# One-core transformer layer: attention weighs two key blocks side by side, takes its denominators from GpSimd sums and gives its score banks out in rotation

## What is computed

```python
kqv = x @ Wqkv + bqkv
kqv = kqv.reshape(b, s, 3, NUM_HEADS, HEAD_SIZE)      # 16 heads of 32
...
scores = jnp.einsum('bsnh,btnh->bnst', k, q) / math.sqrt(HEAD_SIZE)
ones = jnp.ones_like(scores)
scores = jnp.triu(scores) + -10000.0 * jnp.tril(ones, k=-1)
attn = jax.nn.softmax(scores, axis=2)
out = jnp.einsum('bnkq,bknh->bqnh', attn, v)
out = out.reshape(b, s, NUM_HEADS * HEAD_SIZE)
return out @ Wo + bo
```

## Time and profile before

| what | value |
|---|---|
| times of three runs | 3363.21, 3372.99 and 3378.21 us |
| median | 3372.99 us |
| the profiled execution: its own time | 3368.79 us |
| the profiled execution: its span | 3367.1 us |
| mean granted clock of TensorE, as a share of full speed | 0.936 |
| busy shares: PE, DVE, ACT, POOL | 91%, 66%, 33%, 22% |
| attention of the first batch | from about 168 us to 427 us of the span |

### The profile page before, as it was taken

One profiled execution on the slowest core, in us unless ns is written; L12 is line 12 of the kernel. 1 busy time (PEld: TensorE's weight loads), 2 busy tenths in 40 slices (PEclk: granted clock), 3 DMA queues, 4 the chain that ended last, 5 costly groups with the idle time before them and its releaser, 6 DMA issues.

```text
span 3367.1 us, 59590 instructions
## 1 busy us (share of the span) xinstructions
PE 3061.7 (91%) x20772; PEld 2095.2 (62%) x20772; DVE 2211.2 (66%) x2961; ACT 1102.6 (33%) x1728; POOL 752.8 (22%) x1065
## 2 busy tenths in 40 slices
PE   3599999999879998999978999999997999999998
PEld 3445457777555446777755544777774454577775
DVE  1356667777646667777764675777764566677776
ACT  1123314444113333344311332344421233143441
POOL 3301102333031111233311110133322011013330
PEclk6779999999879999999987999999998799999999
DMA  7422202111131211111121220111112222021111
GB/s 229 144 47 69 51 1 64 44 48 56 48 82 44 63 32 34 43 49 51 41 83 44 63 63 14 54 41 48 45 48 77 51 69 51 1 64 43 48 57 48
DMA packets 160038, 189.48 MB, mean 56 GB/s; under 512 B 43834, under 2 KB 103866, under 8 KB 158074
## 3 DMA queue, kind: packets, MB, share of 16 engines
q1 hardware_dynamic: 155998, 173.74, 18.6%
q0 software_dynamic: 2720, 10.49, 0.8%
q10 hardware_dynamic: 1152, 3.15, 0.4%
HBM read 104.90 MB, written 23.36 MB: 38 GB/s over the span
## 4 chain that ended last, share of the span: by engine, by line
PE 76%; DVE 9%; issue 4%; DMA 4%; SPq 3%; ACT 2%; POOL 1%; DVEq 0%; ACTq 0%; POOLq 0%
PE ps L700 13%; PE ps L702 12%; PE ps L701 12%; PE ps L844 7%; PE ps L809 6%; PE ps L827 5%; PE ps L1000 4%; PE ps L886 3%; PE ps L986 2%; PE ps L745 2%; PE ps L1046 2%; DVE LM L1558 2%; PE ps L710 1%; DVE mneg L1466 1%; PE ps L1009 1%
## 5 line engine op out<-in xcount | busy, mean ns | idle before, releaser
L700 PE MATMUL ps<-uh,win 128*128 128x512 f32 x1536 | 629.8, 410 | 4.1 <-POOL win L1719 3.4
L702 PE MATMUL ps<-uh,win 128*128 128x512 f32 x1536 | 605.3, 394 | 0.0
L701 PE MATMUL ps<-ul,win 128*128 128x512 f32 x1536 | 602.4, 392 | 0.0
L1466 DVE TENSOR_REDUCE mneg<-ps 128x1 f32<-128x128 f32 (+7 forms) x512 | 363.5, 752 | 179.1 <-PE ps L812 173.6
L1175 ACT ACTIVATE PR<-ps 128x1024 f32<-128x1024 f32 (+3 forms) x384 | 310.2, 809 | 412.4 <-PE ps L830 275.0
L700 PEld LDWEIGHTS ps<-uh,win 128*128 128x128 f32 x1536 | 290.9, 189 | 95.8 <-issue 29.6
L844 PE MATMUL ps<-PR,VG 128*32 128x512 f32 (+3 forms) x1536 | 339.6, 519 | 10.8 <-DVE OS L1472 8.3
L846 PE MATMUL ps<-PR,ones 128*32 128x512 f32 (+3 forms) x1536 | 339.6, 519 | 0.0
L702 PEld LDWEIGHTS ps<-uh,win 128*128 128x128 f32 x1536 | 290.0, 189 | 65.3
L1582 DVE TENSOR_TENSOR LM<-ps,LM 128x512 f32<-128x512 f32 x256 | 170.2, 686 | 243.1 <-PE ps L1000 197.3
L701 PEld LDWEIGHTS ps<-ul,win 128*128 128x128 f32 x1536 | 291.4, 190 | 54.9
(11 more groups left out here) (216 smaller groups left out, 5162.1 us busy)
## 6 DMA issues: line engine op xcount, KB each, us to landing
...
QS<-EV SPq DMA_DIRECT2D x192, 128.0 KB, 2.4
KS<-EV SPq DMA_DIRECT2D x168, 128.0 KB, 2.4
...
edec<-ed_t SPq DMA_DIRECT2D x512, 16.0 KB, 1.6
```

The lines of the kernel that those rows point to most:

```text
L700: pe.matmul(dst, hi_l, hi_r, start=first, stop=False)
L701: pe.matmul(dst, hi_l, lo_r, start=False, stop=False)
L702: return pe.matmul(dst, lo_l, hi_r, start=False, stop=last)
L1466: dve.tensor_reduce(mneg[:, hh, t:t + 1], wide(b0)[:, 0:(t + 1) * P], AX.X, ALU.max, negate=True).then_inc(a_max.sem, 1)
```

## The change

- `scores_b` now goes through the units in plain order. `weigh` takes two units (a pair, k = 0 to 5) at a time: unit 2k in the column groups 0 and 1, unit 2k+1 in 2 and 3. The products with ones are gone from it. DVE's `take` adds the two parts: one or two copies from PSUM and an addition, for each of the two column halves c.
- POOL adds up the probabilities of a half into `acc` (`sums`, ten steps, each after the unit's exponential), and PE makes the denominators of both column halves from it with four matmuls side by side (`denominators`), once in a half, after pair 0 of the next half; for p7 within `row_product`, after its first row block. ACT copies them to `rec`, DVE inverts them in two steps of 128 x 256 and multiplies (`scale`), which POOL did before. The low part of the weights (`group_lo`) also moves from POOL to DVE.
- PR has four tiles. The exponential of unit u waits for POOL's sum and PE's weighing of unit u-4.
- The banks 0 to 5 are three slots of two banks, given out in rotation to all score jobs: units ("b"), row blocks of `scores_a` ("a", 16 blocks packed into ten jobs by `TILES`) and transposes of maxima ("t"). A job waits for the reader of the job three places ahead of it (`slot_free`).
- The maxima are turned in two steps of 8 rows (t0 and t1); their DMAs, two each, are issued by ACT. The first two units of the next half stand in `TAIL`. SP stacks queries and keys of the next group in two portions.
- The first group and the last stand outside of the loop, which the program before did for the last alone. Semaphores of loads and stores are merged (`s_tile`).

```diff
-ORDER = [(0, 0), (0, 3), (0, 2), (0, 1), (1, 0), (1, 7), (1, 6), (1, 5), (1, 4), (1, 1), (1, 2), (1, 3)]
+ORDER = [(c, s) for c in range(2) for s in range(4 * c + 4)]
 UNITS = len(ORDER)
-
-SCORE_BANK = [2, 4, 2] + [4] * 7 + [2, 4]
-
-BANK_FREE = [-1, 0, 1, 2, 4, 5, 6, 7, 8, 9, 3, 10]
-
-
-AHEAD = {2: (0, 1, 2, 3), 3: (4, 5), 4: (6, 7), 5: (8, 9, 10, 11), 6: (12, 13), 7: (14, 15)}
-TURN_AT = 9
-PROJECT_AT = (4, 6, 8, 10)
-
-MAX_BANK = [0, 1, 2, 3, 0, 2, 0, 2]
-MAX_FREE = [-1, -1, 0, 0, 2, 4, 5, 6]
+PAIRED = UNITS // 2
...
+TILES = [[(0, 3, 0), (0, 2, 512), (0, 0, 896)], [(1, 3, 0), (1, 2, 512), (1, 0, 896)],
+         [(0, 4, 0), (0, 1, 640)], [(1, 4, 0), (1, 1, 640)],
+         [(0, 5, 0)], [(1, 5, 0)], [(0, 6, 0)], [(1, 6, 0)], [(0, 7, 0)], [(1, 7, 0)]]
+
+AT = [[], [("a", 0), ("a", 1)], [("a", 2), ("a", 3), ("a", 4)], [("t", 0), ("a", 5), ("a", 6), ("a", 7)], [("a", 8), ("a", 9)], []]
+TAIL = [("b", 12), ("b", 13), ("t", 1)]
+SUMMED = [1, 1, 2, 3, 4, 4, 5, 6, 7, 8, 9, 10]
...
+BODY = [j for k in range(PAIRED) for j in units_of(k) + AT[k]] + TAIL
+CLOSE = [j for k in range(PAIRED) for j in units_of(k)]
+OPEN = [("a", i) for i in range(5)] + [("t", 0)] + [("a", i) for i in range(5, 10)] + TAIL
...
+            if i >= 3:
+                self.before[j] = (jobs[i - 3], 0)
+            elif earlier:
+                self.before[j] = (earlier[i - 3], 1)
...
-            PR = sb("PR", [P, 2, 2, HB], at=c)
-            mneg = sb("mneg", [P, 2, TT], at=c)
-            mrow = sb("mrow", [2 * TT, P], F32R, at=c)
-            OS = sb("OS", [P, HB], at=c)
+            PR = sb("PR", [P, 4, 2, HB], at=c)
+            mneg = sb("mneg", [P, 2, 2, HALF], at=c)
+            mrows = sb("mrows", [32 + TT, P], F32R, at=c)
+            mrow = [mrows[32 * i:32 * i + TT, :] for i in range(2)]
+            OS = sb("OS", [P, 2, HB], at=c)
             rec = sb("rec", [P, HB], at=c)
+            acc = win_raw[:, 1].rearrange("p w s k n -> p (w s k n)").rearrange("p (c h t) -> p c h t", c=2, h=2)
...
-                def maxima(g, hf):
-                    m_act.wait(sp, b * 8 + g * 2 + hf, 1)
-                    sp.dma_start(QS[hf][STACK:STACK + 1, :, :].bitcast(F32), mrow[:, :].bitcast(F32)).then_inc(s_mrow[hf], 16)
...
+                            st_pe.wait(sp, b * 8 + g * 2, UNITS)
+                            sp.sem_inc(s_tick, 1)
+                            pj_lo.wait(sp, b * 4 + g + 1, 2)
+                            sp.sem_inc(s_tick, 1)
+                            stack(sp, 0, (0,))
                             pj_lo.wait(sp, b * 4 + g + 1, 4)
-                            st_pe.wait(sp, b * 8 + g * 2 + 1, 0)
-                            stack(sp, 0)
-                            maxima(g + 1, 0)
+                            sp.sem_inc(s_tick, 1)
+                            stack(sp, 0, (1,))
...
+                den_pe.wait(sp, b * 8 + 7, 1)
...
+                    if t == 0 and between is not None:
+                        between()
...
+                def slot_free(slots, p, job):
+
+                    if job not in slots.before:
+                        return
+                    (kind, i), back = slots.before[job]
+                    q = p - back
+                    if kind == "b":
+                        ex.wait(pe, q + i // UNITS, i % UNITS + 1)
+                    elif kind == "a":
+                        a_max.wait(pe, q + 1, i + 1)
+                    else:
+                        m_act.wait(pe, q + 1, i + 1)
...
+                def turn_maxima(slots, p, c):
+
+                    a_max.wait(pe, p + 1, 4 if c == 0 else 10)
+                    slot_free(slots, p, ("t", c))
...
-                        i = pe.matmul(ps[r:r + HS, 6, at:at + n], ones[:, 0:HS],
-                                      PR[:, u % 2, hh, 0:n], start=(s == 0), stop=last)
...
+                def weigh(p, hf, k):
+
+                    ex.wait(pe, p, 2 * k + 2)
+                    if k == 0:
+                        o_copied.wait(pe, p, 0)
+                        vg_done.wait(pe, p, 1)
+                    elif k == 2:
+                        o_copied.wait(pe, p, 1)
...
+                            h, o = (2 * hf + hh) * HS, j * 64 + hh * HS
+                            i = pe.matmul(ps[o:o + HS, 6, at:at + n], VG[:, s, h:h + HS],
+                                          PR[:, u % 4, hh, 0:n], start=(k in (0, 2)), stop=(k in (1, 5)))
                     i.then_inc(pv.sem, 1)
+
+                def denominators(p):
+
+                    summed.wait(pe, p, 10)
+                    for c in range(2):
+                        for hh in range(2):
+                            o = c * 64 + hh * HS
+                            i = pe.matmul(ps[o:o + HS, 7, :], ones[:, 0:HS], acc[:, c, hh, :], start=True, stop=True)
+                    i.then_inc(den_pe.sem, 1)
...
+                    for k in range(PAIRED):
+                        for job in units_of(k):
+                            scores_b(slots, p, p, hf, occ, job)
+                        weigh(p, hf, k)
+                        if k == 0 and not (first and hf == 0):
+                            if hf == 1 and not first:
+                                pj_lo.wait(pe, b * 4 + g, 4)
+                            denominators(p - 1)
+                        if not close:
+                            for job in AT[k]:
+                                if job[0] == "t":
+                                    turn_maxima(slots, p, job[1])
+                                else:
+                                    scores_a(slots, p, 1 - hf, occ + hf, job[1])
+                        if hf == 0 and not last and 1 <= k <= 4:
+                            if k == 1 and not first:
+                                den_act.wait(pe, p - 1, 1)
+                            project(g + 1, k - 1)
...
+                        for job in TAIL:
...
+                    act.copy(mrow[c][:, :], ps[0:TT, slots.bank["t", c], 0:P]).then_inc(m_act.sem, 1)
+                    m_act.wait(act, p, c + 1)
+                    for hh in range(2):
+                        act.dma_start(QS[slot][STACK:STACK + 1, hh, c * HB:(c + 1) * HB].bitcast(F32),
+                                      mrow[c][hh * HALF:(hh + 1) * HALF, :].bitcast(F32)).then_inc(s_mrow[slot][c], 16)
...
+                    if u >= 4:
+                        pv.wait(act, p, (u - 4) // 2 + 1)
+                        summed.wait(act, p, SUMMED[u - 4])
+                    elif not first:
+                        pv.wait(act, p - 1, (u + 8) // 2 + 1)
+                        summed.wait(act, p - 1, SUMMED[u + 8])
...
+                def take(p, hf, c):
+
+                    pv.wait(dve, p, 2 if c == 0 else PAIRED)
+                    rows_ = slice(c * 64, (c + 1) * 64)
+                    f = P if c == 0 else 0
+                    if f:
+                        dve.tensor_copy(OS[rows_, hf, 0:f], ps[0:64, 6, 0:f])
+                    dve.tensor_copy(OS[rows_, hf, f:HB], ps[64:128, 6, f:HB]).then_inc(s_half, 1)
+                    dve.wait_ge(s_half, p * 2 + (c + 1))
+                    dve.tensor_tensor(OS[rows_, hf, f:HB], ps[0:64, 6, f:HB], OS[rows_, hf, f:HB], ALU.add).then_inc(o_copied.sem, 1)
+
+                def invert(p, q):
 
                     if q == 0:
-                        o_copied.wait(dve, p, c + 1)
-                    cols = slice(q * HB // parts, (q + 1) * HB // parts)
-                    i = dve.reciprocal(rec[hf * 64:(hf + 1) * 64, cols], OS[(1 - hf) * 64:(2 - hf) * 64, cols])
-                    if q == parts - 1:
-                        i.then_inc(o_rec.sem, 1)
+                        den_act.wait(dve, p, 1)
+                    cols = slice(q * WIN, (q + 1) * WIN)
+                    dve.reciprocal(rec[:, cols], rec[:, cols]).then_inc(o_rec.sem, 1)
...
+                        dve.tensor_tensor(dst, OS[rows_, hf, :], rec[rows_, :], ALU.mult).then_inc(o_scaled.sem, 1)
...
+                    for k in range(1, 5):
+                        if not close:
+                            for kind, i in AT[k]:
+                                if kind == "a":
+                                    maximum(SLOTS_BODY, p + 1, i)
+                        if k == 1:
+                            take(p, hf, 0)
+                        if hf == 0 and not last:
+                            project_lo(g + 1, k - 1, False)
+                        if k <= 2 and not head:
+                            invert(p - 1, k - 1)
+                        if k == 2 and not head:
+                            scale(p - 1, g if hf == 1 else g - 1, 1 - hf)
...
+                        until(den_pe, p - 1, 1)
+                    for u in (1, 2, 3, 5, 6, 7, 8, 9, 10, 11):
+                        c, s_, t0, n = span(u)
+                        at = t0 - c * HB
+                        until(ex, p, u + 1)
+                        if u == 1:
+                            pool.tensor_copy(acc[:, 0, :, 0:P], PR[:, 0, :, 0:P]).then_inc(s_add, 1)
```

(9 more changed lines are left out.)

331 lines of the change are left out of this document (179 added, 152 removed).

## The result

| what | before | after |
|---|---|---|
| median of the runs | 3375.6 us (4) | 3507.4 us (4) |
| lowest and highest | 3363.21, 3379.02 | 3492.57, 3513.88 |
| profiled execution: its own time, its span | 3368.79, 3367.1 us | 3492.57, 3491.0 us |
| mean granted clock | 0.936 | 0.901 |

What follows compares the result with a forecast made beforehand. PE was taken as the bound, with DVE close behind. A batch summed -6 + 1.7 - 4 + 4.1 + 2 = -2.2, times four -9; with +19 for the clock, 3383 us, range 3290 to 3445.

Steps and rivals of the forecast that it cites:

- The two multiplications come from POOL: 2 x 0.65: DVE's work in a half: the multiplications taken over from POOL add 1.3 us, for a net of -0.5.
- the prediction's own timetable: Half without projections: PE until a0 8.5, DVE 16.0, PE 2.2, so a period of 26.7 us against 25.0 before.
- rival D: GpSimd, contending with DVE over SBUF, sets the period of a half: 28.6 us, in all 3445; chance 0.10.
- 17.5 + 2.7 + 1.3: POOL's run in a half: sums 17.5 us, handovers 2.7, and 1.3 for DVE's multiplications beside it.
- I take a fall in every third of these 20 halves ... 6.8 us of low clock: TensorE's clock in halves without projections: about 2.7 us lost in each of 7 falls, +19 us.
- The upper bound of +68: Clock falls in each of the 20 halves without projections, 3.4 us of PE's work each: +68 us.
- Rival C: The clock falls in every half without projections, decided at the take's 2.3 us wait: 3432 us; chance 0.15.
- a half with projections fills the waits: Halves with projections: their matmuls fill the waits and keep most of PE's 3.0 us, so -2.5 us each.
- The opening: Start of a batch, from first row block to unit 0, 17.7 us before: 4 us less.
- The wait of p7's product: In p7's product with Wo, PE waits about 3.4 us for POOL's sums, which may cost the high clock.
- The end: End of a batch, p7 and its product with Wo: +4.1 us as POOL sets the end, +2 for the clock.
- Rival B: PE's own work stays the bound: halves without projections take 22.5 us, in all 3280 to 3320; chance 0.30.

Runs made afterwards that it cites:

- both edits: Against the changed kernel: multiplications moved to the start of the half after, and DVE's take of c = 0 ahead of a0 and a1's maxima; 3314.76 us, 0.9825.

## Why the prediction was wrong

**The step that failed first: "The two multiplications come from POOL: 2 x 0.65".** They took 2.0 and 2.1 us on average (L1609, 64.0 and 66.7 us for 32 each), 4.87 in p3. That is 2.8 us a half on average, 3.6 in p3, in a stretch where, by the prediction's own timetable, DVE was the pace. The mechanism of the timetable held, and this term of it was mis-sized. The rival D had seen that the engines contend there, with the Trainium skill (GPSIMD Engine Reference, "8. Key points"), which names DVE instructions with two SBUF inputs: here the trace agrees, since the take's addition with one operand in PSUM kept its 0.55 us and the inversions their 1.74 beside the same sums, and L1609 was stretched. But the prediction, like the select of the earlier trace rows, put the cost on GpSimd (1.3 us in "17.5 + 2.7 + 1.3"). In the earlier trace rows the select had started second, 0.44 us behind the addition, and the one that starts second pays, as the last section shows; in the changed kernel the multiplications start second. The earlier trace rows had the DVE side too, 1.34 us for an addition that takes 1.23 elsewhere; it was not weighed, and by its size (+9%) would have been too small a bound.

**The second: "I take a fall in every third of these 20 halves ... 6.8 us of low clock".** In the kernel after, every half from p1 to p6 of the first batch had low clock, 6.8 to 17.1 us each, 260 us more in all. The upper bound of +68 supposed 6.8 us of it in a half; with the waits of 3 us that the multiplications added it fell for longer. The price depends on what sets the half. With late multiplications, in halves alike but for the added matmuls, it is 29.3 us with 10.2 low and 25.4 with none. In the kernel after, the fall behind the take's wait hides behind VectorE's chain (32.3 us with it, 32.2 without), and the one behind the last maxima is paid: 1.8 us in p3, 3.0 in p4. Rival C (3432) had the mechanism and the place of the first fall, the take's wait; but in p3 of the kernel after that fall is not what costs.

**The third: GpSimd late in halves with projections.** The prediction's "a half with projections fills the waits" took for granted that p2 and p4 don't depend on POOL. The exponential of unit 4 does, through `acc` and the place of the denominators: 1.2 to 1.8 us of PE's wait, and 1.5 us of such a half, 3.0 where the clock fell behind it.

**What held.** The weighing of 512 columns at 1.00 us. The timetable of p3 up to T = 20: unit 4 at 6.3 (5.7 forecast), pair 2 at 13.2 (13.1), the wait for the take 1.85 (2.3). POOL's sums:

```profile
L1905 POOL TENSOR_TENSOR win_raw<-win_raw,PR 128x1024 f32<-128x1024 f32 x96 | 228.2, 2377 | 97.0 <-ACT PR L1256 78.2 <-POOL win_raw L1905 18.8
```

The opening gained: 184.19 - 170.06 = 14.1 us from the first row block to unit 0, against 17.7, so -3.5 for the -4. The wait of p7's product, 2.03 in after with the clock low ahead of it and 3.89 in the kernel with both edits, for 3.4. The end, from p7's first unit to the last product with `Wo`, came to 480.23 - 426.45 = 53.8 us for 453.92 - 405.59 = 48.3 before: +5.5, for +4.1 + 2. That is close in part by luck, since p7 itself waits 1.31 and 2.52 us for exponentials, which the sum did not have.

Rival B's outcome came with both edits, not by its rule: "each microsecond that a0 is earlier is one off the period". In p3 of that kernel VectorE's maxima begin at 9.6 us, later than the 9.1 in after; what got shorter is the chain from there to a7, 11.8 us for 19.2. p6 then takes 23.7 us, less than the 25.0 before.

The change gives 2 to 2.5% once VectorE's new work stands in another order; in the order that it had, it lost 4. And about half of what the kernel with both edits gains on the kernel before lies in p0: in the first batch 9.5 of 20.5 us, where TensorE has 6.5 us of low clock instead of 18. No run separates what brings the clock back earlier there.

**How the loss adds up.** From 3507 us: 114 by the place of the multiplications, of the rest 79 by the take's, of which 53 also by filling TensorE's wait, and then about 68 by GpSimd's sums, of which the place of the denominators gave back 13 to 27. The parts overlap, and only their order here gives these sizes; the 13 to 27 are differences of medians whose intervals overlap. How much of the 260 us of added low clock is paid for in the kernel after is not known in all: one of its falls was shown to cost nothing in p3, another to cost 3.0 us in p4.
